# A four-DMA read-back moved from ScalarE's queue to SyncE's queue, with two instead of three swap and transpose buffers

## The reference

```python
re = xe * c - xo * s                      # xe, xo: even and odd features of a head
ro = xe * s + xo * c
...
q = _rope(_heads(xq @ wq), sq, cq)
k = _rope(_heads(ctx @ wk), sk, ck)       # self-attention: ctx is xq
a = softmax(einsum('bhnd,bhmd->bhnm', q, k) * DH ** -0.5)
o = einsum('bhnm,bhmd->bhnd', a, v)       # DH = 64, 16 heads
x = o @ wo + bo + x
...
x = gelu(adaln(x) @ ff_w1 + ff_b1) @ ff_w2 + ff_b2 + x
```

## Time and profile before

| what | us |
|---|---|
| median of three runs | 4023.44 |
| the profiled execution | 4023.44 |
| its span, first to last instruction | 4021.6 |
| TensorE busy in the span | 3839.9 |
| VectorE busy | 3162.7 |
| GpSimd busy | 2863.8 |
| ScalarE busy | 2469.6 |

### The profile page before, as it was taken

One profiled execution on the slowest core, in us unless ns is written; L12 is line 12 of the kernel. 1 busy time (PEld: TensorE's weight loads), 2 busy tenths in 40 slices (PEclk: granted clock), 3 DMA queues, 4 the chain that ended last, 5 costly groups with the idle time before them and its releaser, 6 DMA issues.

```text
span 4021.6 us, 92934 instructions
## 1 busy us (share of the span) xinstructions
PE 3839.9 (95%) x32822; PEld 3295.6 (82%) x32822; DVE 3162.7 (79%) x6610; ACT 2469.6 (61%) x10244; POOL 2863.8 (71%) x2674
## 2 busy tenths in 40 slices
PE   7999999999989999999999999899999999999999
PEld 6777777777779997888888888778888888878998
DVE  7888889899885547888888888898898989985443
ACT  6999998898883334555555555465555555554333
POOL 5777877777767777666666666577777777766776
PEclk9999999999999999999999999999999999999999
DMA  2011111111111113777767677777677777772110
GB/s 81 28 33 33 33 46 48 34 49 49 53 40 53 43 64 103 219 212 220 217 212 220 208 223 226 213 216 231 220 225 225 219 229 224 229 229 82 53 43 32
DMA packets 415216, 544.98 MB, mean 136 GB/s; under 512 B 58524, under 2 KB 311968, under 8 KB 414752
## 3 DMA queue, kind: packets, MB, share of 16 engines
q1 hardware_dynamic: 267228, 404.74, 30.6%
q10 hardware_dynamic: 147524, 134.30, 13.1%
HBM read 220.11 MB, written 184.55 MB: 101 GB/s over the span
## 4 chain that ended last, share of the span: by engine, by line
PE 69%; DVE 12%; ACT 7%; POOL 5%; issue 3%; DMA 2%; ACTq 1%; SPq 0%; DVEq 0%; POOLq 0%
PE BANKS L621 17%; PE BANKS L622 15%; PE BANKS L623 15%; PE BANKS L780 6%; PE BANKS L768 5%; ACT PR L926 4%; PE BANKS L701 3%; PE BANKS L816 3%; POOL PR L1265 2%; PE BANKS L838 2%; DMA PB<-p_scratch 1%; DVE WL L1118 1%; DVE PT L1073 1%; DVE SN L1146 1%; POOL Z L1310 1%
## 5 line engine op out<-in xcount | busy, mean ns | idle before, releaser
L1265 POOL TENSOR_TENSOR PR<-PR,RL 128x512 f32<-128x512 f32 x1024 | 1066.9, 1045 | 575.7 <-DVE RL L1078 571.2
L942 ACT ACTIVATE PR<-BANKS,NM 128x128 f32<-128x128 f32 x2048 | 719.4, 378 | 360.9 <-DVE NM L1132 360.3
L926 ACT ACTIVATE PR<-BANKS,NM 128x128 f32<-128x128 f32 x2048 | 728.5, 414 | 12.6 <-DVE NM L1065 10.5
L621 PE MATMUL BANKS<-HH,WH 128*128 128x512 f32 x1632 | 681.1, 417 | 1.6 <-ACT HF L969 1.6
L622 PE MATMUL BANKS<-HL,WH 128*128 128x512 f32 x1632 | 642.5, 394 | 0.0
L623 PE MATMUL BANKS<-HH,WL 128*128 128x512 f32 x1632 | 641.4, 393 | 0.0
L926 ACT ACTIVATION_READ_ACCUMULATOR PR<-BANKS,NM 128x1 f32 x2048 | 520.9, 255 | 0.0
L933 ACT ACTIVATE OH<-BANKS 128x512 fp32r<-128x512 f32 x256 | 153.0, 598 | 480.3 <-PE BANKS L768 256.5
L942 ACT ACTIVATION_READ_ACCUMULATOR PR<-BANKS,NM 128x1 f32 x2048 | 445.0, 217 | 0.0
L1132 DVE TENSOR_REDUCE NM<-BANKS 128x8 f32<-128x1024 f32 x256 | 309.4, 1208 | 149.7 <-PE BANKS L780 148.0
L1270 POOL TENSOR_TENSOR HL<-HF,HH 128x512 fp32r<-128x512 f32 x192 | 256.3, 1335 | 217.9 <-DVE HH L1026 203.8
(11 more groups left out here) (134 smaller groups left out, 10691.8 us busy)
## 6 DMA issues: line engine op xcount, KB each, us to landing
SW<-SN SPq DMA_DIRECT2D x1024, 128.0 KB, 2.9
p_scratch<-TR SPq DMA_DIRECT2D x256, 512.0 KB, 4.6
PB<-p_scratch ACTq DMA_DIRECT2D x1024, 128.0 KB, 3.7
x_scratch<-X SPq DMA_DIRECT2D x80, 512.0 KB, 3.2
X<-x_scratch SPq DMA_DIRECT2D x80, 512.0 KB, 4.3
CX<-in_ctx SPq DMA_DIRECT2D x32, 384.0 KB, 4.4
X<-in_x SPq DMA_DIRECT2D x16, 512.0 KB, 4.0
out<-X SPq DMA_DIRECT2D x16, 512.0 KB, 2.9
```

The costliest lines, as they stand in the source:

```text
L621: e.matmul(o, lh, rh, start=first and i == 0, stop=False)
L926: made = e.activation(pr[:, r], bank[:, r], ACT.Exp, bias=nm[:, h:h + 1], accum_out=RL[npr(t)[0]][:, h:h + 1])
L942: made = e.activation(pr[:, r], bank[:, r], ACT.Exp, bias=nm[:, h:h + 1], accum_out=RL[npr(t)[0]][:, h:h + 1])
L1265: e.tensor_tensor(p3, p3, RL[npr(t)[0]][:, :].unsqueeze(2).broadcast_to([128, 4, 128]), ALU.mult).then_inc(s_nrm, 1)
```

## The change

Four things change, all but the last in the two `b` stages.

1. The get is issued by SyncE instead of ScalarE, at T+5 instead of T+6. In that tick it stands ahead of the q swap. Its two waits stay the same: the put's landing, and the P V product of three units before.
2. SW has two buffers instead of three. Swap r now waits for addition r-2.
3. TR has two buffers instead of three. The transpose of unit x waits for the landing of the put of unit x-2.
4. Memory is laid out anew (SW0, TR0, TR1, SW1; the shared area is 5632 instead of 6656 floats a partition), and 2048 instead of 256 bytes are set aside for DMA descriptors that GpSimd would write.

```diff
--- before.py
+++ after.py
@@ -16,7 +16,7 @@
 NSTG = 3
 NH = 3
 NP0, NPT0 = 5, 6
-NP1, NTR, NSW, NPT1, NSC = 4, 3, 3, 3, 4
+NP1, NTR, NPT1, NSC = 4, 2, 3, 4
 
 CONTEXT = ("Wk", "Wv", "ck", "cv")
 
@@ -196,7 +196,7 @@
                 for j in range(8):
                     x = Unit(unit, p, g, j)
                     tick = tg + 2 * j
-                    for stage, lag in (("q1", -5), ("q1_add", -3), ("k1", -4), ("k1_add", -2), ("scores", 0), ("max", 0), ("put", 4), ("get", 6),
+                    for stage, lag in (("q1", -5), ("q1_add", -3), ("k1", -4), ("k1_add", -2), ("scores", 0), ("max", 0), ("put", 4), ("get", 5),
                                        ("pv", 8), ("low", 8), ("out", 9)):
                         at[stage, tick + lag].append(x)
                     at["v1", tick + 1].append((p, g, j))
@@ -281,9 +281,10 @@
             PT = [sb(f"PT{i}", [128, 512], stack=soft) for i in range(NPT0)]
         with spare:
             sb("PR_L1", [128, 512 * NP1], stack=spare)
-            SW = [sb(f"SW{i}", [128, 512], stack=spare) for i in range(NSW)]
+            SW = [sb("SW0", [128, 512], stack=spare)]
             TR = [sb(f"TR{i}", [128, 1024], stack=spare) for i in range(NTR)]
-        sb("SHARED", [128, 512 * (NP1 + NSW + 2 * NTR)])
+            SW += [sb("SW1", [128, 512], stack=spare)]
+        sb("SHARED", [128, 512 * (NP0 + NPT0)])
         CX = sb("CX", [128, G, 256])
         PB = [sb(f"PB{i}", [128, 4, 256]) for i in range(NPT1)]
         with first:
@@ -351,7 +352,7 @@
             sem(k) for k in ("s0", "nm0", "s", "nm", "exp", "rl", "nrm", "t", "pt_a", "pt_d", "pv0", "pv"))
         s_oh, s_ol, s_y = sem("oh"), sem("ol"), sem("y")
         s_qk, s_rt, s_zz, s_v1, s_va = (sem(k) for k in ("qk", "rt", "zz", "v1", "va"))
-        s_sw = [sem(f"sw{i}") for i in range(NSW)]
+        s_sw = [sem(f"sw{i}") for i in range(2)]
         s_tr = sem("tr")
         s_put = [sem(f"put{i}") for i in range(NTR)]
         s_get = [sem(f"get{i}") for i in range(NPT1)]
@@ -592,13 +593,19 @@
                     q.wait_ge(s_tr, 2 * x.i + 2)
                     q.wait_ge(s_pv, x.i - NSC + 1)
                     e.dma_start(PSC[x.i % NSC], TR[x.i % NTR][:, :]).then_inc(s_put[x.i % NTR], 16)
+                for x in at["get", tick]:
+                    q.wait_ge(s_put[x.i % NTR], 16 * (x.i // NTR + 1))
+                    q.wait_ge(s_pv, x.i - NPT1 + 1)
+                    turned = PSC[x.i % NSC].rearrange("(i c) (j k) -> j c i k", i=4, j=4)
+                    for j in range(4):
+                        e.dma_start(PB[x.i % NPT1][32 * j:32 * j + 32, :, :], turned[j]).then_inc(s_get[x.i % NPT1], 16)
                 for w, stage in enumerate(("q1", "k1")):
                     for x in at[stage, tick]:
                         r = 2 * x.i + w
                         q.wait_ge(s_rt, r + 1)
-                        q.wait_ge(s_zz, r - NSW + 1)
+                        q.wait_ge(s_zz, r - 1)
                         for i in range(2):
-                            e.dma_start(SW[r % NSW][i:128:2, :], SN[r % 2][1 - i:128:2, :]).then_inc(s_sw[r % NSW], 16)
+                            e.dma_start(SW[r % 2][i:128:2, :], SN[r % 2][1 - i:128:2, :]).then_inc(s_sw[r % 2], 16)
                 done = [(x.p, x.g) for x in at["res0", tick] if x.b == G - 1]
                 done += [(x.p, x.g) for x in at["out", tick - 1] if x.j == 7]
                 done += [(p, g) for p, g, j in at["down", tick - 1] if j == 7]
@@ -886,13 +893,6 @@
                     e.dma_start(CROWB[r + 1:r + 2, 64 * i:64 * i + 64], a[key][128:CD].unsqueeze(0)).then_inc(s_crows, 16)
 
             for tick in ticks:
-                for x in at["get", tick]:
-                    q.wait_ge(s_put[x.i % NTR], 16 * (x.i // NTR + 1))
-                    q.wait_ge(s_pv, x.i - NPT1 + 1)
-                    turned = PSC[x.i % NSC].rearrange("(i c) (j k) -> j c i k", i=4, j=4)
-                    for j in range(4):
-                        e.dma_start(PB[x.i % NPT1][32 * j:32 * j + 32, :, :], turned[j]).then_inc(s_get[x.i % NPT1], 16)
-
                 for p, g, j in at["q_high", tick]:
                     ga = xq(p, g)
                     q.wait_ge(s_q, 2 * ga + j + 1)
@@ -1142,7 +1142,7 @@
                         q.wait_ge(s_rope, 16)
                         e.tensor_tensor((QT, KT)[w][x.i % 3][:, :].rearrange("p (b t) -> p b t", b=G), src, cs, ALU.mult)
                         if r >= 2:
-                            q.wait_ge(s_sw[(r - 2) % NSW], 32 * ((r - 2) // NSW + 1))
+                            q.wait_ge(s_sw[r % 2], 32 * (r // 2))
                         e.tensor_tensor(SN[r % 2][:, :].rearrange("p (b t) -> p b t", b=G), src, sn, ALU.mult).then_inc(s_rt, 1)
 
                 for x in at["low", tick]:
@@ -1280,8 +1280,8 @@
                     for x in at[stage, tick]:
                         r, z = 2 * x.i + w, (QT, KT)[w][x.i % 3]
                         q.wait_ge(s_rt, r + 1)
-                        q.wait_ge(s_sw[r % NSW], 32 * (r // NSW + 1))
-                        e.tensor_tensor(z[:, :], z[:, :], SW[r % NSW][:, :], ALU.add).then_inc(s_zz, 1)
+                        q.wait_ge(s_sw[r % 2], 32 * (r // 2 + 1))
+                        e.tensor_tensor(z[:, :], z[:, :], SW[r % 2][:, :], ALU.add).then_inc(s_zz, 1)
 
                 for p, g, j in at["up", tick]:
                     f = ffj(p, g, j)
@@ -1349,7 +1349,7 @@
     import concourse.bacc as bacc
     from concourse.bass_utils import run_bass_kernel_spmd
 
-    nc = bacc.Bacc("TRN2", target_bir_lowering=False, num_devices=1, dynamic_dma_scratch_size=256)
+    nc = bacc.Bacc("TRN2", target_bir_lowering=False, num_devices=1, dynamic_dma_scratch_size=2048)
     arrays, aps = {}, {}
     for name, arr in [(n, inputs[n]) for n in _INS] + list(_constants().items()):
         arr = np.ascontiguousarray(arr)
```

## The result

The changed kernel takes 4079.31 us, the median of four runs (4074.68 to 4083.11), against 4023.93 us for the kernel before: a ratio of 1.0138, 95% interval 1.012 to 1.0155. That is 55 us slower. I had forecast slower by 18 us.

The account below looks back on a forecast made before the run. TensorE's pace was taken as the bound, 7.95 and 7.92 us a unit in the two stages. Terms 15 + 10 - 7 = +18 us on 4023.44 gave 4041 us, range for 8 in 10 from 4006 to 4105.

Parts of the forecast that it names:

- the larger of the two costs in the sum: Get on SyncE: +15 us for waiting inside SyncE's queue; the other cost was +10 us for two SW buffers.
- the circle on SyncE: SyncE's queue: put issued, landed, four gets, q swap, next put; 7.7 and 7.8 us a plain unit, taken as +15 us.
- -7 for TensorE's waits: Both b stages: an earlier get would win 7 of the 10.8 us that TensorE waits for PB.
- The threshold of 4.83 us in the mean: Mean put landing up to which SyncE's put-to-put sequence closes in time; each 0.1 us above costs 25.6 us.
- upper bound of 20.6: Two SW buffers: at most a second time TensorE's 20.6 us of waits for KT in the second stage.
- halve the term: Two SW buffers: +10 us, half of 20.6, since half the waits fall at group starts, where splits hold GpSimd.
- The sum: 15 + 10 - 7 = +18 us on 4023.44 us, giving 4041 us; chance 0.38.
- SyncE's circle binds: Rival: SyncE's queue binds throughout at a mean put landing of 5.1 us, 69 us plus 10, about 4100 us; chance 0.18.
- Faster: Rival: mean put landing below about 4.5 us, PB waits go (10.8 us), OL waits lose 3; about 4010 us; chance 0.22.

## Why the prediction was wrong

The direction was right and the size was not, and the direction was partly luck: the larger of the two costs in the sum did not occur. By the steps of the prediction:

- **Change 1, the get on SyncE**, was put at +15 us for the circle on SyncE and -7 for TensorE's waits. It is -12 alone (0.997). The step that failed is the landing time of a put. I took 4.6 and 4.7 us from the kernel before and left open whether it would fall; with the move alone it is 3.9 and 3.7 us in the median, and in the mean over the same puts 4.2 and 3.8. The threshold of 4.83 us in the mean was right as arithmetic, and the landing stayed below it. Why it fell is not shown: the move changes the queue and also brings the get forward by a tick, and no run has the get at T+5 on ScalarE. By issues and landings in the traces a put has a get under way beside it for 3.5 and 3.2 us in the mean before, 1.8 and 1.5 with the move alone and 2.6 and 2.0 with two SW buffers alone, and the mean landings stand in the same order (4.9 and 4.6, 4.2 and 3.8, 4.5 and 4.1). That fits less company on the DMA engines as the reason, and the get still runs beside the next put for a part of it. On the gain side the wait for PB went as forecast, 8 of 9.3 us in the second stretch, but other waits of TensorE took its place there and TensorE's busy time stayed the same. That the 12 us are those waits is not shown.
- **Change 2, two SW buffers**, was put at +10 us with an upper bound of 20.6. It is +89 alone (1.0225) and the whole of the loss in the changed kernel. The failed step is how I looked for the price. I worked out one q swap in the middle of a group, where it was held for 0.3 us and the get covered it, and never the k swap, which is held for 3.6 us in the stretch shown and was not held before. I had even named the splits that hold GpSimd at the start of a group, but as a reason to halve the term. What I didn't do is follow the wait back: the addition that a k swap now waits for stands in the same tick as the swap, behind a split. The trace of the kernel before had the price: at the start of a group the product of k ends at 1985.11 and the addition that a second buffer would need at 1988.65, 3.5 us later. The upper bound was a wait of TensorE in the kernel before, once more, and that bounds nothing: three buffers had kept the late split away from the k swap, so no wait of that kernel held its price.
- **Change 3, two TR buffers**, 0 forecast, 0 measured (0.9998). With the move it is the same, 4014.64 us with three and 4015.07 with two. VectorE did wait for puts in the changed kernel, 22.0 us in the second stretch, without a cost that the runs can tell.
- **Change 4, layout and descriptor area**, 0 forecast. No run has it alone. The third SW buffer back gives the whole loss back with another layout (0.9968), and the wait alone in the old layout costs as much as the buffer (1.0218), so nothing is left for it to explain.
- **The sum** of +18 was two wrong terms: -12 instead of +8 for the move, and +64 instead of +10 for the ring once the move is made (4079 us with two SW buffers against 4015 with three).
- **The rivals.** "SyncE's circle binds" would have been the nearest in time, 4100 us, and its mechanism didn't occur. "Faster" was right for the move alone in the landing and in the wait for PB, but not in the wait for OL, which grew. None of them had the late split.
- The Trainium skill's rule that the issuing engine matters only for the issue time, page "DMA: Bandwidth & Descriptors", section "Issuing engines are not separate DMA queues", stood in the prediction for a move that costs nothing. It came nearer to the 12 us gained than my sum. It says nothing of the order in time that a queue imposes, and here the puts landed 0.7 and 1.0 us sooner after the move; whether the queue or the earlier tick did that, no run here shows.

## What to carry to other kernels

When a ring gets shorter, write down for each step that waits (here for the k swap as well as the q swap) which step of which engine frees the buffer, in which tick, and what stands ahead of that step on its engine; follow it until it ends or closes. A delay that a longer ring kept apart costs nothing in the profile before, so the waits there don't bound its price, and the place to look is where extra work enters the queues, here the splits for the next group. Such a dependence can be cheaper to cut by the order of two steps on one engine than by memory: the additions ahead of the splits made the two-buffer ring free, and the kernel 15 us faster even with three.

## What the runs showed that I had not expected

The place of the get among the puts moves a put's landing: with the move alone the median fell from 4.6 to 3.9 us for the same 512 KB at the same rate (217 against 216 GB/s in the first stretch), and from 4.7 to 3.7 at 226 GB/s in the second. And the time that a DMA takes on the issuing queue isn't fixed: the four gets at 1992.28 took 3.56 us, where about 1.9 is the median. Nearly all of the excess is in one of the four:

```profile
1992.86 2.03 SPq L601 DMA_DIRECT2D PB<-p_scratch  x1
```
